# Adjacency column sums of layer 0 moved from the recurrent network's steps into the graph convolution

## The reference, cut to what matters

```
def _L0_gnn_ref(x, adj, W_rel, b_rel, W_root, ln_gamma, ln_beta):
    h = layer_norm(x, ln_gamma, ln_beta)
    agg = jnp.einsum('bij,bjh->bih', adj, h)
    conv = jnp.einsum('bkh,ho->bko', agg, W_rel) + b_rel + jnp.einsum('bkh,ho->bko', h, W_root)
    return x + jax.nn.relu(conv)
...
def step(carry, xs):                       # _L0_ffn_ref, 128 steps, state 64 x 128
    h, c = carry
    xi_t, xf_t, xg_t, xo_t = xs
    i_t = jax.nn.sigmoid(xi_t + h @ V_i)
    g_t = jnp.tanh(xg_t + h @ V_c)
    o_t = jax.nn.sigmoid(xo_t + h @ V_o)
    c_new = h * c + i_t * g_t
    h_new = o_t * jnp.tanh(c_new)
...
def _L1_gnn_ref(x, adj, weight, bias):
    adj_norm = adj / (jnp.sum(adj, axis=-1, keepdims=True) + EPS)
    h_neigh = jnp.einsum('bnm,bmf->bnf', adj_norm, x)
```

## Time and profile before

| what | value |
|---|---|
| median of 3 runs | 1869.44 us (1867.5 to 1871.53) |
| profiled execution, first to last instruction (its span) | 1867.1 us |
| the same execution outside its span | not listed apart; its span is 2.3 us under the median |
| granted TensorE clock, mean over the span | 0.941 |
| layer 0's convolution | from the start to about 109 us |
| the recurrence | about 111 to 406 us |
| TensorE busy over the span | 1627.8 us (87%) |

### The profile page before, as it was taken

How to read it: one execution, slowest core, us unless ns; L and a number is a source line. 1 busy time by engine, 2 the same in 40 slices (tenths; PEclk the granted TensorE clock), 3 DMA queues, 4 the chain that set the end, 5 groups by cost and what they waited for, 6 DMA issues and landing times. The chain is left out here.

```text
span 1867.1 us, 43356 instructions
## 1 busy us (share of the span) xinstructions
PE 1627.8 (87%) x13366; PEld 1314.2 (70%) x13366; DVE 1095.9 (59%) x4199; ACT 998.9 (53%) x3116; POOL 786.7 (42%) x1358
## 2 busy tenths in 40 slices
PE   7978899988859987999998888879999888884995
PEld 5756677767759985788887566679999845553542
DVE  7933433348737777699998755523333377763552
ACT  5854444446636656666665433246666534441663
POOL 6710000014426666111111677745565434554675
PEclk9989999999969999899999799989999989995998
DMA  3200000010014420000000511122222253105331
GB/s 114 84 1 1 1 1 1 1 27 1 1 36 134 123 80 1 2 3 2 2 3 3 156 47 48 62 62 70 72 71 72 56 150 86 58 24 88 100 86 35
DMA packets 125926, 91.76 MB, mean 49 GB/s; under 512 B 23591, under 2 KB 116554, under 8 KB 125701
## 3 DMA queue, kind: packets, MB, share of 16 engines
q1 hardware_dynamic: 109110, 61.89, 12.6%
q0 software_dynamic: 13568, 25.90, 4.3%
q10 hardware_dynamic: 3024, 1.21, 0.4%
HBM read 57.71 MB, written 33.30 MB: 49 GB/s over the span
## 5 line engine op out<-in xcount | busy, mean ns | idle before, releaser
L1361 ACT ACTIVATE FEAT<-BANKS,FEAT 128x128 f32<-128x128 f32 x544 | 155.5, 368 | 82.1 <-PE BANKS L1314 82.1
L1206 POOL DMA_INDIRECT scratch_made<-FEAT x136 | 144.9, 1065 | 122.6 <-DVE FEAT L1500 119.8
L1061 ACT ACTIVATE EXP<-BANKS,NEGMAX 128x128 f32<-128x128 f32 x512 | 139.4, 383 | 59.5 <-DVE NEGMAX L1073 59.5
L440 ACT ACTIVATE gates<-BANKS,EXP 128x64 f32<-128x64 f32 x384 | 97.4, 314 | 112.6 <-PE BANKS L417 112.6
L1314 PE MATMUL BANKS<-FEAT 128*128 128x128 f32 x1088 | 145.5, 277 | 0.0
L1323 PE MATMUL BANKS<-AUX,FEAT 128*128 x1088 | 144.5, 276 | 0.4 <-ACT FEAT L1361 0.4
L417 PEld LDWEIGHTS BANKS<-AUX,EXP 128*128 128x128 f32 x768 | 95.4, 191 | 69.7 <-DVE AUX L464 69.6
L1198 POOL DMA_INDIRECT scratch_sent<-FEAT,POS x128 | 125.1, 977 | 38.3 <-issue 37.5
L990 POOL COPY EXP<-AUX 128x32 f32<-128x32 f32 x256 | 42.5, 211 | 217.8 <-PE BANKS L1036 217.8
L1314 PEld LDWEIGHTS BANKS<-FEAT 128*128 128x128 f32 x1088 | 133.9, 194 | 0.0
L1323 PEld LDWEIGHTS BANKS<-AUX,FEAT 128*128 128x128 f32 x1088 | 133.2, 193 | 0.6 <-issue 0.6
(11 more groups left out here) (367 smaller groups left out, 4196.0 us busy)
## 6 DMA issues: line engine op xcount, KB each, us to landing
EXP<-in_L_ffn_W SPq DMA_DIRECT2D x128, 128.0 KB, 2.1
FEAT<-scratch_sent SPq DMA_DIRECT2D x136, 64.5 KB
EXP<-scratch_made SPq DMA_DIRECT2D x32, 256.0 KB, 3.4
FEAT<-scratch_sent SPq DMA_DIRECT2D x96, 65.5 KB, 1.9
X<-in_x SPq DMA_DIRECT2D x16, 256.0 KB, 2.9
STAGE<-in_adj SPq DMA_DIRECT2D x16, 256.0 KB, 3.3
scratch_sent<-NONE SPq DMA_DIRECT2D x48, 65.5 KB, 3.3
scratch_sent<-FEAT,POS POOLq DMA_INDIRECT x192, 2.3
```

Of the source, the lines that this page charges most:

```text
L440: act.activation(gates[:, at, sp_, :], PS[2 * at + par][:, u * B:(u + 1) * B], f, bias=wr["b" + gate]).then_inc(done, 1)
L1061: last = act.activation(tile(EXS[:, par], 4 * k + n), tile(PS[j], c), ACT.Exp, bias=NEGMAX[:, par, 4 * k + n:4 * k + n + 1])
L1206: pool.indirect_dma_start(out=made2, out_offset=bass.IndirectOffsetOnAxis(ap=XI_I[:, t % R_IN, H:ROW2], axis=0), in_=YO[:, t % R_OUT, :], ...
L1361: last = act.activation(tile(HR[:, t % R_H], c), tile(PS[2 + t % 2], c), ACT.Gelu, bias=BT[:, c, t:t + 1])
```

## The change

The 64 products of an `AT` tile with a column of ones leave the recurrence. Each group's `conv` in layer 0 now issues four of them, behind the four products with `AT` and behind the increment of `s.conv`. In the recurrence the number of fillers no longer depends on the step: two where L407 runs, three elsewhere.

```diff
@@ -217,6 +217,7 @@
         adj_v = a["adj"].rearrange("(g b) i j -> g i b j", b=G)
         x_v = a["x"].rearrange("(g b) t h -> g t b h", b=G)
+        ROWSUM = PS[6][:, 0:B]
         PWB = sb("PWB", [P, 2, 2, 2, G])
@@ -368,6 +369,8 @@
                                          start=False, stop=True, skip_group_check=True)
                     last.then_inc(s.conv, 1)
+                    for k in range(G):
+                        pe.matmul(ROWSUM[:, G * i + k:G * i + k + 1], cols(AT, i, GW, k * T, T), ones[:, 0:1], start=True, stop=True)
 
                 def back(i, par, half):
@@ -419,9 +421,7 @@
                             inputs(j + 1, 1 - par, u // 2, u % 2)
-                        if step < B:
-                            pe.matmul(ROWSUM[:, step:step + 1], AT[:, step * T:(step + 1) * T], ones[:, 0:1], start=True, stop=True)
-                        for _ in range((2 if prefetch and u < 6 else 3) - (step < B)):
+                        for _ in range(2 if prefetch and u < 6 else 3):
                             pe.matmul(PS[7][:, 0:half], ident[:], cols(FEAT, j, STEPS * B, 0, half), start=True, stop=True)
```

More of the change, by code:

```diff
@@ L392, in program @@
         NT = T // STEPS
-        ROWSUM = PS[6][:, 0:B]
         with nc.Block() as block:
```

## The result

The changed kernel took 1878.94 us (median of 4 runs, 1877.41 to 1881.69) against 1870.01 us for the kernel before (4 runs beside it, 1867.5 to 1871.53): a ratio of 1.0050, 95% interval 1.0036 to 1.0064. It is slower by some 9 us. The forecast was 1880.7 us, range 1875.5 to 1885.

What follows compares the result with a forecast made beforehand. Layer 0 was taken as bound by a 5.39 us ring through ScalarE and TensorE, the recurrence by its 2.27 us step chain. 15 rounds x 0.75 = 11.2 us, recurrence 0: 1869.4 + 11.2 = 1880.7 us, range 1875.5 to 1885.

Steps and rivals of the forecast that it cites:

- the ring: Layer 0: ScalarE's L308, L313, L319, then TensorE's WE transposes, root product and convolution set the 5.39 us round.
- 0.33 us a round to spare: Layer 0: VectorE, busy 5.06 us a round, has 0.33 us to spare now and 1.08 after the change.
- The price of the column products: Layer 0, behind each convolution: eight weight loads 0.111 us apart cost 0.89 us of TensorE's time.
- What is hidden: Layer 0: WA transposes are 0.14 us early, so 0.75 of 0.89 us shows, making a round 6.14 us.
- The sign: Layer 0, changed profile: a wait of some 0.7 us ahead of L313's counterpart, released by the WA transposes.
- The uncovered end: Layer 0: 15 rounds pay; behind the last convolution the WD loads' 0.97 us wait covers the 0.89.
- The recurrence: 64 steps swap two narrow records for two wide ones in TensorE's wait; step stays 2.27 us, gain 0, loss 0.
- Hidden columns: Layer 0: the eight records fit in 0.14 us or L313 is late anyway; no change, 1869 to 1872, chance 0.07.
- Shorter steps: Recurrence: 64 steps shorten, 6.4 us per 0.1 us a step; faster overall needs 0.23 us each; chance 0.03.
- A late clock rise on top: Recurrence start: first steps run at 1.2 GHz for two steps more, +3.2 us, so 1883.9; chance 0.08.
- the main case: Whole kernel: the forecast of 1879 to 1883 us, given a chance of 0.72.
- a part hidden: Layer 0: part of the column products' cost is hidden, leaving 5 to 9 us, 1875 to 1878; chance 0.10.

Runs made afterwards that it cites:

- e7: The changed kernel with the WE transposes issued one round later (lag 5 instead of 4): ratio 1.0014 to the kernel before.
- e6: The kernel before with the WE transposes issued one round later (lag 5 instead of 4): ratio 0.9999.
- e3: The changed kernel with one filler less in each of recurrence steps 0 to 63: ratio 1.0049 to the kernel before.
- e2: The kernel before, column products left in the recurrence, with one 256-column filler more in each of steps 0 to 63: ratio 0.9991.
- e1: The changed kernel with each group's four column products issued behind the next group's WA transposes, ahead of the WD transposes: 1866.68 us against 1867.74, ratio 0.9995.
- e4: The changed kernel with each group's four column products issued twice at the same place: 1894.55 us, ratio 1.0143 to the kernel before.

## Why the prediction was right, point by point

- **What bounds layer 0.** Right: the ring through L308, L313, L319, WE and the convolution. e7 cut it and the round fell from 6.10 to 5.50. One sentence was too generous: VectorE was said to have 0.33 us a round to spare, from its busy time of 5.06. e6 and the row of the kernel before show that its queue ran at 5.36 a round without an idle, so it had 0.03 to spare, and with the prediction's 6.14 it would have had 0.78, not 1.08. Busy time leaves out the small gaps between its instructions (in e6's timeline 0.10 us between L172 and the L176 that reads its result). It changed nothing, since the round only grew.
- **The price of the column products.** Right in kind: the two ends of the table give (6.99 - 5.65) / 12 loads = 0.112 us a record, and eight loads of 128-column products (L359 in the earlier trace rows) take the same 0.97 us as the eight of one-column products. The Trainium skill's rule that spoke against a cost (page "TensorE: Matmul & The Clock Gate", section on the back-to-back issue gap, some 25 ns for a matmul of so few columns) isn't what ruled here; by its section on LDWEIGHTS, P / 1.2 ns, a load of 128 columns takes 107 ns, which agrees. That it is the load that takes this time, and not something else in the pair of load and product, isn't shown: no run here issues products without a load for each.
- **What is hidden.** Mis-sized by 0.04 us: 0.14 forecast, 0.18 measured by the table; hence 0.71 a round and not 0.75, 10.6 us and not 11.2. The term of the sum that was too large is the 8 x 0.111 = 0.89 us: in the timeline the new products go ahead of the WA transposes by 62.28 - 61.46 = 0.82 us. Seven spacings of 0.111 us lie between the eight loads, but the WA load starts only 0.04 behind the eighth (62.17 against 61.35 + 0.97 - 0.19 = 62.13). The WA transposes then take 0.64 instead of 0.60, which returns half of that. The sign was named as a wait of some 0.7 us; the bracket has 0.60, since it is counted from the relu's end, and L313 used to start 0.10 ahead of that end (52.47 against 51.88 + 0.69).
- **The uncovered end.** Right: 15 rounds paid, and behind the last convolution the WD loads, 0.97 us of wait before, have none now and start as far behind the relu as they did:

```profile
110.14 0.97 PEld L373 LDWEIGHTS BANKS<-ones,AT 128*128 128x128 f32 x8
...
110.44 0.69 ACT L309 ACTIVATE WD<-BANKS,w_b 128x512 f32<-128x512 f32 x1 [0.72 <-PE BANKS L369]
111.18 0.42 PEld L195 LDWEIGHTS BANKS<-ident,WD 128*128 128x128 f32 x4
```

- **The recurrence.** Right: 0. The step is 2.27 us with one filler less (e3), with the change, and with the column product beside the change's fillers (e2). The 0.015 us by which the second half's mean step was longer was left out of the sum as single late instructions. In the changed kernel the second half again takes 146.1 / 64 = 2.28 and the first, with the same fillers, 2.27, so it wasn't the fillers' doing. Three late steps (last section) make all of it. The start was named as near 122 and came at 120.80: 10.1 us later than before, which is the 10.6 less the 0.6 of the first relu. The prediction's "twelve input products" at 0.40 apiece are six products in twelve records; the sums with them hold, since they count records.
- **The rivals.** Hidden columns: the round of 6.10 us rules it out. Shorter steps: none. A late clock rise on top: the rise came some 0.9 us earlier against the input products, not later, and gave 0.5 us back, within the 2.2 us that the prediction allowed for that.
- **The total.** 11.2 us forecast, 8.9 and 9.7 measured in two comparisons. 0.6 of the difference is the mis-sized term; the rest lies within the intervals, and the profile's items above (first relu 0.6 earlier, input products 0.5 faster, later stages 1.0 to 1.4 less) are of the size by which executions of the same stages differ. The total alone would not have settled the matter: 1878.94 us lies just under the main case (1879 to 1883), and a price of 8.9 us is inside that of the case "a part hidden" (5 to 9 us). It is the round, 6.10 us against 6.14, that tells them apart.

## What to carry to other kernels

A piece of work moved out of a stage where it was free need not be free elsewhere: look at what stands behind it in the queue and how early that is, here 0.18 us against 0.89. On a full-looking engine there can be a hole of the right size one instruction group further on, and moving the same work there (e1) made the whole loss go away. To find the hole, follow the ring of waits through one round, and take the neighbours' pace from the distance of their instructions, not from their busy time.

## What the runs showed of the hardware that was not expected

- **The clock fell under a TensorE that the records call busy.** In e4 a round's 16 records of one column and eight transposes ran from 105.20 to 107.97 us, TensorE busy for 2.77 of 2.80 us at clock 1.00; then the granted clock was 0.73 over 108 to 110 and 0.61 over 110 to 113. The changed kernel, with eight such records a round, kept 1.00 in all eleven rounds; but so did e4 itself with sixteen from 30 to 100 us, so what the fall answered to isn't shown. It also fell once near the start of e4, to 0.50 over 24 to 26.
- **The same steps are late each time.** In all ten traces of this document the new states of three steps come late, some 2.47, 2.64 and 2.62 us behind the one before instead of 2.27: the 66th, the 84th and the 102nd. Together that is 0.9 us, the whole of 64 x 0.015. In the kernel before, the cell's instruction of one step in the second half (the 84th) started with 0.47 us of idle time ahead of it where the others have none, at 305.40; in the changed kernel the same happens at 315.04, the step with the same number, 9.6 us later. So it isn't chance. Its cause wasn't looked for.

```profile
305.40 0.22 DVE L461 TENSOR_TENSOR cell<-hc,ig 128x64 f32<-128x64 f32 x1 [0.47 <-DVE ig L458]
```

```profile
315.04 0.22 DVE L461 TENSOR_TENSOR cell<-hc,ig 128x64 f32<-128x64 f32 x1 [0.47 <-DVE ig L458]
```
